# Last frequency mixing of a four-layer kernel: alternating column groups, quarter units in a ring of four, staging copies by DMA

## What is computed

```python
def _L3_conv_ref(x, weights):
    x_f = jnp.fft.rfft2(x)
    k_f = jnp.fft.rfft2(weights)
    out_f = jnp.einsum('bchw,ochw->bohw', x_f, k_f)
    return jnp.fft.irfft2(out_f, s=(H, W))

x = x + _L0_conv_ref(_gn(x), L0_conv_weights_r, L0_conv_weights_i)
x = x + _L1_conv_ref(_gn(x), L1_conv_gain)
x = x + _L2_conv_ref(_gn(x), L2_conv_weight)
x = x + _L3_conv_ref(_gn(x), L3_conv_weights)
```

## Time and profile before

| | us |
|---|---|
| median of 3 runs (1042.07 to 1048.86) | 1047.77 |
| the profiled execution | 1046.7 |
| its span in the trace | 1044.6 |
| mixing stage, first instruction to last matmul | 819.8 to 945.9 |
| TensorE busy on L1600 | 115.1 |

### The profile page before, as it was taken

The page is one execution under the profiler, slowest core; times in us unless marked ns, Lnnn a source line. Parts: engine busy times, 40 slices in busy tenths (PEclk is TensorE's granted clock), DMA queues, the critical chain, the costliest instruction groups (busy, mean ns, idle before and its releaser), DMA issues. The chain is left out here.

```text
span 1044.6 us, 26773 instructions
## 1 busy us (share of the span) xinstructions
PE 867.7 (83%) x10199; PEld 739.5 (71%) x10199; DVE 661.8 (63%) x1208; ACT 521.8 (50%) x900; POOL 122.4 (12%) x120
## 2 busy tenths in 40 slices
PE   6999999775467956488759999994888789998998
PEld 6999999764367854276534444444777689998998
DVE  3555464675585668868966867766656788871232
ACT  2444444476434327265459999103877322325555
POOL 0000000001001005335600231100000100001110
PEclk9999999899688988888969999996999999999999
DMA  6465757373400010000000000004000347740222
GB/s 254 163 241 180 279 205 244 103 174 77 97 9 1 0 24 13 0 1 0 0 1 1 2 1 1 1 1 91 6 0 0 82 83 161 157 84 1 100 107 114
DMA packets 48004, 79.89 MB, mean 76 GB/s; under 512 B 19386, under 2 KB 37952, under 8 KB 45136
## 3 DMA queue, kind: packets, MB, share of 16 engines
q1 hardware_dynamic: 31312, 62.39, 21.4%
q10 hardware_dynamic: 16640, 16.78, 4.6%
HBM read 50.65 MB, written 27.92 MB: 75 GB/s over the span
## 5 line engine op out<-in xcount | busy, mean ns | idle before, releaser
L1475 DVE SCALAR_TENSOR_TENSOR X<-bank,c_power,X 32x512 f32 x128 | 95.9, 749 | 42.2 <-PE bank L1426 38.6
L1600 PE MATMUL bank<-m_xp,m_kf 128*32 128x64 f32 x2048 | 115.1, 223 | 8.8 <-DVE m_xp L1568 6.6
L1600 PEld LDWEIGHTS bank<-m_xp,m_kf 128*32 128x32 f32 x2048 | 114.7, 139 | 9.3 <-issue 9.3
L926 DVE TENSOR_TENSOR X<-X,bank 128x512 f32 x64 | 43.7, 682 | 92.3 <-PE bank L912 92.3
L205 DVE BATCH_NORM_STATS2 bn<-X 128x6 f32 x128 | 85.4, 686 | 2.9 <-POOL X L1214 1.6
L1616 ACT COPY xm<-bank 64x512 f32 x64 | 32.5, 584 | 95.9 <-PE bank L1600 95.9
L1380 ACT ACTIVATE c_r<-X,c_nrm 32x1024 f32 (+1 forms) x56 | 74.4, 1329 | 2.4 <-DVE c_nrm L1449 1.1
L441 DVE COPY ks_cols<-bank 128x512 f32<-128x512 f32 x64 | 42.7, 683 | 45.9 <-PE bank L407 45.9
L355 ACT COPY ks_spec<-bank 128x512 f32<-128x512 f32 x64 | 37.5, 587 | 65.2 <-PE bank L415 30.7
L438 DVE COPY ks_tt<-bank 128x512 f32<-128x512 f32 x64 | 42.3, 689 | 43.7 <-PE bank L381 43.7
L388 PE MATMUL bank<-ks_fw,ks_tt 128*128 128x128 f32 x512 | 64.6, 277 | 0.0
(11 more groups left out here) (193 smaller groups left out, 2102.4 us busy)
## 6 DMA issues: line engine op xcount, KB each, us to landing
ks_src<-in_L_conv_weights SPq DMA_DIRECT2D x32, 512.0 KB, 5.7
kf<-ks_spec ACTq DMA_DIRECT2D x16, 1024.0 KB, 8.8
m_kf<-kf SPq DMA_DIRECT2D x32, 512.0 KB, 8.0
X<-in_x SPq DMA_DIRECT2D x4, 2048.0 KB, 11.6
out_y<-X SPq DMA_DIRECT2D x16, 512.0 KB, 2.7
xf<-f_xm SPq DMA_DIRECT2D x6, 448.0 KB
l_wb<-in_L_conv_weights_r SPq DMA_DIRECT2D x4, 512.0 KB, 12.8
l_wb<-in_L_conv_weights_i SPq DMA_DIRECT2D x4, 512.0 KB, 14.4
```

The lines of the kernel that those rows point to most:

```text
L926: dve.tensor_tensor(x, x, ps[4 + c % 4][:], ALU.add).then_inc(added, 1)
L1475: dve.scalar_tensor_tensor(x, of.rearrange("p (y x) -> p y x", x=HN), filt.power[at, 2:3], x, ALU.mult, ALU.add).then_inc(added, 1)
L1600: last = pe.matmul(ps[4 * half + m // 8][at:at + C, m % 8 * N:(m % 8 + 1) * N], kf[p][:, j, :, H * half + m], xp[half][:, j, m].rearrange( ...
```

## The change

In `l3_mix_stage`:

- The unit of work is a quarter of the columns (16 frequencies) instead of a half, 32 products, and `m_xp` is four buffers of half the size, used in a ring. `mixed` counts units.
- Inside a unit the two column groups alternate product by product.
- The plain copy of the real rows goes, for three of the four quadrants, to DMAs from SBUF to SBUF on SyncE's queue (32 partitions of 2 KB each); ScalarE does the fourth. VectorE keeps the negation and the imaginary copy.
- ScalarE stages one quadrant of a unit, then reads the results of the unit two before it, and it issues the weight loads.
- The weights of a phase are loaded by one DMA over 128 partitions. For that `kf` has another layout, and the store in `kernel_spectra_stage` is four DMAs of 32 partitions instead of two of 128.

```diff
-        self.kf = nc.dram_tensor("kf", (SLOT // 4, P, 2, C // IB, IB * N), F32, kind="Internal").ap()
+        self.kf = nc.dram_tensor("kf", (SLOT // 4, 2, C, 4, C // IB, IB * N), F32, kind="Internal").ap()
...
-                        for part in range(2):
-                            act.dma_start(pr.kf[:, :, part, 2 * i + p, :].rearrange("s p n -> p s n"),
-                                          spec[:, :, part].rearrange("p s o k -> p s (o k)")).then_inc(stored, 16)
+                        for g in range(4):
+                            act.dma_start(pr.kf[:, :, :, g, 2 * i + p, :].rearrange("s r c n -> c (s r) n"),
+                                          spec[g * C:(g + 1) * C].rearrange("p s r o k -> p (s r) (o k)")
+                                          ).then_inc(stored, 16)
...
+def load_kernel_spectra(eng, pr, to, i, pair, loaded):
+
+    eng.dma_start(to[:].rearrange("p j o k -> p (j o k)"),
+                  pr.kf[bass.ds(2 * i, 2)].rearrange("s r c g t n -> (s r c) (g t n)")[
+                      :, pair * 2 * C * N:(pair + 1) * 2 * C * N]).then_inc(loaded, 16)
...
+        xp = [pr.sb(ctx, f"m3_xp{u}", [P, 2, 2, U, 2 * B]) for u in range(4)]
...
+                with sp.Fori(0, PAIRS) as i:
                     for p in range(2):
...
+                        for u in range(4):
+                            sp.wait_ge(mixed, START + UNITS * i + 4 * p + u - 3)
+                            for j, s2 in ((0, 0), (0, 1), (1, 0)):
+                                sp.dma_start(real(u, j, s2), spectrum(i, p, u, j, s2).rearrange("p k r b -> p k (r b)")
+                                             ).then_inc(re_moved[u], 16)
...
+                def stage(i, p, u):
+
+                    for j, s2 in np.ndindex(2, 2):
+                        of, to = spectrum(i, p, u, j, s2), imaginary(u, j, s2)
+                        dve.tensor_scalar(to[:, :, 0:B], of[:, :, 1, :], -1.0, None, ALU.mult)
+                        last = dve.tensor_copy(to[:, :, B:2 * B], of[:, :, 0, :])
+                    return last
...
+                        pe.wait_ge(loaded[p], 16 * i + 16)
+                        for u in range(4):
+                            n = UNITS * i + 4 * p + u
+                            pe.wait_ge(re_moved[u], 2 * MOVED * i + MOVED * (p + 1))
+                            pe.wait_ge(re_copied, n + 1)
+                            pe.wait_ge(im_staged, n + 1)
+
+                            pe.wait_ge(mixed_read, START + n - 3)
+                            pe.sem_inc(pr.pace, 1)
+                            for m in range(U):
+                                for j in range(2):
                                     at = (2 * p + j) * C
...
+                                                     kf[p][:, j, :, U * u + m], xp[u][:, j, :, m],
                                                      start=True, stop=True)
...
+                def group(i, first, more):
+                    for l in range(UNITS):
+                        p, u = l // 4, l % 4
+                        if not first or p:
+                            act.wait_ge(mixed, START + UNITS * i + l - 3)
+                        stage(i, p, u)
+                        if l >= 2:
+                            read(i, (l - 2) // 4, (l - 2) % 4)
+                        elif not first:
+                            read(i - 1, 1, l + 2)
+                        if l == 1 and not first:
+                            load_kernel_spectra(act, pr, kf[1], i, 1, loaded[1])
+                        if l == 5 and more:
+                            load_kernel_spectra(act, pr, kf[0], i + 1, 0, loaded[0])
```

More of the change, by code:

```diff
@@ L1557, in _ @@
+            @block.gpsimd
+            def _(pool):
+                for u in (2, 3):
+                    clear(pool, u).then_inc(cleared, 1)
             @block.vector
             def _(dve):
[L1559 to L1562, removed]
-                    stage(dve, 0, 0, half, (0,)).then_inc(fix, 1)
-                    dve.wait_ge(fix, 3 * half + 1)
-                    dve.memset(xp[half][0:C, 0, 0, 0, B:2 * B], 0.0).then_inc(fix, 1)
-                    dve.memset(xp[half][C:2 * C, 0, 0, 0, 0:B], 0.0).then_inc(fix, 1)
-                    dve.tensor_copy(xp[half][C:2 * C, 0, 0, 0, B:2 * B], xm[0:C, 0, H * half, 1, :]).then_inc(staged, 1)
-                    stage(dve, 0, 0, half, (1,)).then_inc(staged, 1)
@@ L1570, in _ @@
-                for half in range(2):
-                    dve.wait_ge(mixed, START + half + 1)
-                    stage(dve, 0, 1, half).then_inc(staged, 2)
+                def stage(i, p, u):
[4 more added lines that the diff above has]
+                    return last
@@ new lines, in pack @@
+                def pack(u):
+                    dve.memset(real(u, 0, 0)[:, 0, B:2 * B], 0.0)
+                    dve.memset(imaginary(u, 0, 0)[:, 0, 0:B], 0.0)
+                    return dve.tensor_copy(imaginary(u, 0, 0)[:, 0, B:2 * B], xm[0:C, 0, U * u, 1, :])
+                for p in range(2):
+                    for u in range(4):
+                        if p:
+                            dve.wait_ge(mixed, START + u + 1)
+                        if p == 0 and u < 2:
+                            clear(dve, u).then_inc(cleared, 1)
+                        last = stage(0, p, u)
+                        if p == 0 and u % 2 == 0:
+                            last.then_inc(fix, 1)
+                            dve.wait_ge(fix, u // 2 + 1)
+                            dve.wait_ge(re_moved[u], MOVED)
+                            last = pack(u)
+                        last.then_inc(im_staged, 1)
@@ L1608, in _ @@
                 act.sem_inc(mixed_read, START)
[L1609 to L1618 removed]
+                load_kernel_spectra(act, pr, kf[1], 0, 1, loaded[1])
@@ new lines, in stage, with read @@
+                def stage(i, p, u):
+                    act.copy(real(u, 1, 1), spectrum(i, p, u, 1, 1).rearrange("p k r b -> p k (r b)")
+                             ).then_inc(re_copied, 1)
+                def read(i, p, u):
+                    act.wait_ge(mixed, START + UNITS * i + 4 * p + u + 1)
+                    at = slice(p * 2 * C, (p + 1) * 2 * C)
+                    for h in range(2):
+                        k = U * u + 8 * h
+                        c = act.copy(xm[at, bass.ds(2 * i, 2), k:k + 8].rearrange("p s k r b -> p k s (r b)"),
+                                     ps[2 * u + h][at, :].rearrange("p (k s n) -> p k s n", s=2, n=2 * B))
+                    c.then_inc(mixed_read, 1)
@@ L1621, in matrices @@
+                group(0, True, True)
+                with act.Fori(1, PAIRS - 1) as i:
+                    group(i, False, True)
+                group(PAIRS - 1, False, False)
+                for u in (2, 3):
+                    read(PAIRS - 1, 1, u)
 def matrices(pr, ctx, shapes, dt=F32):
```

83 lines of the change are left out of this document (26 added, 57 removed).

## The result

| | before | after |
|---|---|---|
| median of 7 runs each, us | 1046.54 | 1053.60 |
| lowest to highest | 1042.07 to 1049.43 | 1051.21 to 1059.06 |
| span of the profiled execution | 1044.6 | 1051.8 |

The ratio is 1.008, 95% interval 1.0057 to 1.0103: slower by 0.8%, where 1003 us were forecast.

The account below looks back on a forecast made before the run. TensorE's matmul stream was taken to bound the mixing, VectorE close behind. 1046.7 - 44.9 (mixing end) - 1.0 (last reads) + 1.5 (first stage) = 1002.3, stated as 1003 us; range 997 to 1011, 8 in 10 within 992 to 1021.

Parts of the forecast that it names:

- 1.5 allowed: First stage: 1.5 us added to the time, for a late store slowed further by loads beside it.
- The two more issues a tile (0.5 each) lie in ScalarE's gaps.: First stage: two further store DMA issues a tile, 0.5 us each, fit into ScalarE's idle time.
- The landing: First stage: a tile's stores in four DMAs of 32 partitions land after 13.5 us, hidden by six tiles.
- the slower rival: First stage: quartered stores too slow, under 105 GB/s, hold up ScalarE and TensorE; 1064 us at 25 us each, chance 0.03.
- Alternation: Mixing matmuls: two column groups run side by side, so instructions start every 29 ns instead of 55, phase 7.5 us.
- If starts stay in order and only the second instruction of one product overlaps the first of the next: Mixing matmuls: this overlap halves the stream time; 27.5 ns an instruction, 29.5 with 2 ns on top.
- VectorE: Mixing: eight operations of 256 elements a unit, starts 0.21 and 0.29 us apart, 2.0 us a unit, phase 8.0.
- SyncE's issues: Mixing: three staging DMA issues at 0.47 us, 1.4 us a unit, phase 5.6.
- Staging by DMA: Mixing: staging DMAs land in 2.0 to 4.5 us, mostly hidden, at worst a few tenths a unit.
- The rival "staging is late so that a unit takes 3.1": Mixing: late staging makes phases 12.3 us, time 1025; part of the rival that DMAs carry less, chance 0.22.
- Weight load: Mixing: one DMA over 128 partitions takes 9 us; TensorE waits about 3.5 us on weights every two phases.
- Start: Mixing start: clearing, staging, slowing and packing put the first matmul near 828, 1.5 us later than before.

## Why the prediction was wrong

The forecast was 1003 us, and the change 44 us faster; it is 7 us slower. By the traces the miss is 22.7 us ahead of the mixing (24.2 lost for 1.5 allowed) and 30.1 in it (81.2 us from its start to its last matmul forecast, 111.3 taken).

**The first stage, the step that failed first:** "The two more issues a tile (0.5 each) lie in ScalarE's gaps." I multiplied the mean of the earlier trace rows, 1.07 us for two, by the number. Four took 4.7 to 7.7, and behind them were the row copies. The gaps took up 4.7 to 5.8 us of it in four tiles, but not the 7.15 to 7.68 of the other three. The step did not ask what stands right behind the issues in the queue. The trace of before had a warning, on SyncE's queue: four DMAs of 100 KB, in runs of 100 bytes, behind a load of `X`.

```profile
150.99 14.79 SPq L1243 DMA_DIRECT2D c_raw<-in_L_conv_weight  x4
```

The landing, for which I worked out 13.5 us and on which the slower rival rests, was 9.2 and cost nothing. So that rival had the right edit and the right sign and the wrong mechanism: it is the issue, not the landing. Repaired in two ways (SyncE's queue, spread issues), the stage ends at 204.6 and 205.6 instead of 223.0.

**Alternation:** the mechanism was right, the term mis-sized. 55 ns became 39.5, not 29. The rule of the Trainium skill ("TensorE: Matmul & The Clock Gate", The mechanism) that a weight load overlaps running matmuls only when its row group differs does not hold here. All products use all rows, and with neighbouring weights an instruction starts every 28.9 ns, while its 64 columns alone take 26.7 (64/2.4 GHz, counted as in the prediction): that leaves no room for a weight load that runs by itself. The step that failed is "If starts stay in order and only the second instruction of one product overlaps the first of the next": it counted columns, and left out that the 32 weights lie 64 elements apart. With neighbouring weights 28.9 ns were measured. I did not look up how the weights of the comparison rows lie.

**VectorE** was right: its operations start 0.21 and 0.29 us apart, 2.0 a unit. **SyncE's issues** took 0.53 each, 1.6 a unit, for 1.4.

**Staging by DMA, the second step that failed:** "So it is mostly hidden; at its worst it costs a few tenths a unit." I gave it 2.0 to 4.5 us to land, from single loads, and it took 4.7 in the median and 8.3 at most beside a weight load. With 1.6 of issuing that is 9.9, more than the 7.6 us of three units. In a phase that waits it costs 2.6 us, 0.65 a unit, and 0.7 more by the clock. The rival "staging is late so that a unit takes 3.1" had the mechanism, at 12.3 a phase; 13.1 were measured where TensorE waits, 10.1 to 10.7 of them matmuls, and 12.3 in the mean of all eight (98.1/8). That the mean meets the rival's figure is luck: it took the matmuls for 7.5.

**Weight load:** its landing was right, the wait on it was not. 9 us were forecast, the seven took 7.3 to 9.6 (median 8.6). The rule of the Trainium skill that 32 neighbouring partitions reach half the DMA ports ("SBUF — State Buffer", Door 1: The DMA port swizzle) pointed to a faster load over 128, and the 8.6 us agree, where 14 were worked out for 205 GB/s. But no wait fell on it: two phases took 26.3 us (891.29 to 917.57), so a load of 8.6 with its 1.6, behind a phase of 10.1, is hidden. I took for the bound what would have been one only at 7.5 us a phase.

**Start:** 8.2 us to the first matmul were forecast, 13.2 taken. The term left out is the wait for the first staging DMA before VectorE may pack (4.3 us). The load of the second weight buffer ran beside it; issued later, it left TensorE a wait of 7.0 instead of 10.8.

**The chances.** Slower was given 0.03, from one mechanism alone. What was missing is a case for ScalarE's queue, where the change added issues ahead of urgent work on the first stage's path.

## What to carry to other kernels

Price DMA issues from a row in which as many of the same kind are issued one behind the other, and look at what stands behind them on their engine: four stores with 1 KB rows cost up to 7.7 us of the queue, the same four apart 1.6, four loads with 4 KB rows 1.9. Small transfers that a ring of buffers waits for must be priced beside the large ones that will run with them. And once an engine gets faster, ask what the next bound is before counting its gain: here 29% less matmul time (115.1 to 82.0 us) gave 12% less of the stage (126.1 to 111.3), and with still faster matmuls nothing more came.

## What the runs showed of the hardware

- Four stores with rows of 1 KB, 512 KB each, issued one right behind the other hold the queue: 4.6 to 7.7 us in all on ScalarE's or SyncE's queue, with shapes of 128 or 32 partitions, the longest where a 2 MB load had been issued 2 us before; two of 1 MB take 1.07. In the run with spread stores the third and the fourth, issued 3.5 to 5 us behind the one before, take 0.32 each. Four loads of 512 KB with 4 KB rows take 1.88 in a row. What limit is met wasn't found; it is not the landing of the first.
- A float32 weight load of 32 columns with elements 256 bytes apart takes 172 ns in the trace and lets the instructions of alternating products start every 37.8 to 39.5 ns; with neighbouring elements 129 ns, and 28.9 at the full clock. DMA traffic makes little of this: at clock 1.00 the changed kernel has 171 instructions in the 6 us from 862 (DMA share 0.29) and 141 in the 5 us from 883 (0.91), so 28 in a microsecond either way (such counts take in the instructions under way at both ends).
- Behind waits of 2.6 to 5 us TensorE's granted clock was 0.50 for the first 2 to 4 us of matmuls and 1.00 after; with no wait (the run without reloads) it stayed at 1.00.
- Staging DMAs of 64 KB between places of SBUF land in 2.0 us (median) in the run without reloads. With a 2 MB load for each phase the median is 4.1 to 5.3 where it comes in one piece over 128 partitions (2.8 in the run without alternation, whose matmuls leave more time between the DMAs), 4.0 in four such pieces, and 7.4 in four pieces of 32 partitions.
